# Cross attention in steps of four chunks, each chunk's copy out of PSUM divided by bank between ScalarE and VectorE

## What is computed

```python
# x: (8, 64, 2048), ctx_4096: (8, 1601, 2048), all float32
def _L0_xattn_ref(query, key):
    a = jnp.einsum('bqd,bkd->bqk', query, key)
    e = jax.nn.softmax(a, axis=-1)
    return jnp.einsum('bqk,bkd->bqd', e, key)

x = x + _L0_xattn_ref(_layernorm(x, axis=-1), ctx_4096)
x = x + _L0_attn_ref(_layernorm(x, axis=-1), L0_attn_w_q, L0_attn_w_k, L0_attn_w_v, L0_attn_w_o)
x = x + _L0_ffn_ref(_layernorm(x, axis=-1), L0_ffn_A_w, L0_ffn_B_w, L0_ffn_Wq_w, L0_ffn_keys)
```

## Time and profile before

| | |
|---|---|
| time, median of 3 runs | 1732.3 us (1731.9 to 1732.43) |
| profiled execution | 1732.83 us, of which the span 1731.0 us |
| PE busy | 1671.8 us, 97% |
| DVE busy | 561.0 us, 32% |
| ACT busy | 455.4 us, 26% |
| mean granted clock | 0.991 |

### The profile page before, as it was taken

The page is one execution under the profiler, slowest core; times in us unless marked ns, Lnnn a source line. Parts: engine busy times, 40 slices in busy tenths (PEclk is TensorE's granted clock), DMA queues, the critical chain, the costliest instruction groups (busy, mean ns, idle before and its releaser), DMA issues.

```text
span 1731.0 us, 21539 instructions
## 1 busy us (share of the span) xinstructions
PE 1671.8 (97%) x9037; PEld 1225.1 (71%) x9037; DVE 561.0 (32%) x1018; ACT 455.4 (26%) x630; POOL 372.5 (22%) x95
## 2 busy tenths in 40 slices
PE   4899999999999979999999999999999999999999
PEld 3555555555555538888888888888888788887877
DVE  2444646465463451101202203112012022138423
ACT  1233332332333232231121221222212212232221
POOL 0000000000001002344344344343343343350010
PEclk9899999999999989999999999999999999999999
DMA  9166675756677533323223323322332342220023
GB/s 339 41 208 189 206 223 172 233 175 217 210 223 230 181 127 122 98 73 97 86 84 97 89 84 95 93 87 84 97 95 75 97 145 74 97 98 25 25 73 122
DMA packets 178882, 224.51 MB, mean 130 GB/s; under 512 B 4240, under 2 KB 102544, under 8 KB 176048
## 3 DMA queue, kind: packets, MB, share of 16 engines
q1 hardware_dynamic: 178816, 223.56, 40.9%
HBM read 212.54 MB, written 11.01 MB: 129 GB/s over the span
## 4 chain that ended last, share of the span: by engine, by line
PE 93%; DVE 2%; SPq 2%; ACT 1%; DMA 1%; issue 1%; DVEq 0%; ACTq 0%
PE ps L761 19%; PE ps L763 18%; PE ps L762 18%; PE ps L635 11%; PE ps L671 10%; PE ps L701 10%; PE ps L1485 2%; SPq L366 2%; PE ps L1599 1%; PE ps L1506 1%; DMA xa_xq<-in_x 1%; PE ps L644 1%; PE ps L1454 0%; PE ps L1492 0%; PE ps L674 0%
## 5 line engine op out<-in xcount | busy, mean ns | idle before, releaser
L1069 POOL TENSOR_TENSOR w_lo<-raw,w_hi 128x2048 fp32r<-128x2048 f32 x75 | 345.1, 4601 | 648.1 <-ACT w_hi L1121 648.1
L761 PE MATMUL ps<-h_hi,w_hi 128*128 128x512 f32 x800 | 316.8, 396 | 0.0
L763 PE MATMUL ps<-h_hi,w_lo 128*128 128x512 f32 x800 | 312.0, 390 | 0.0
L762 PE MATMUL ps<-h_lo,w_hi 128*128 128x512 f32 x800 | 311.7, 390 | 0.0
L1305 DVE TENSOR_TENSOR rows<-rows,ps 128x512 f32<-128x512 f32 x128 | 87.9, 687 | 427.6 <-PE ps L763 427.6
L761 PE MATMUL ps<-w_hi,o_hi 128*128 128x512 f32 x528 | 208.4, 395 | 6.1 <-ACT sa_q_t L1156 4.1
L585 DVE COPY xa_ct<-ps 128x768 f32<-128x768 f32 (+1 forms) x128 | 126.8, 990 | 256.7 <-PE ps L635 172.9
L1121 ACT ACTIVATE w_hi<-raw 128x2048 fp32r<-128x2048 f32 x75 | 143.5, 1913 | 240.4 <-PE ps L763 240.4
L763 PE MATMUL ps<-w_hi,o_lo 128*128 128x512 f32 x528 | 206.2, 391 | 0.0
L762 PE MATMUL ps<-w_lo,o_hi 128*128 128x512 f32 x528 | 206.1, 390 | 0.0
L671 PE MATMUL ps<-xa_ct,xa_q_t 128*64 128x384 f32 x1024 | 202.4, 506 | 0.0
(11 more groups left out here) (205 smaller groups left out, 1529.8 us busy)
## 6 DMA issues: line engine op xcount, KB each, us to landing
xa_raw_a<-in_ctx SPq DMA_DIRECT2D x32, 1536.0 KB
xa_raw_b<-in_ctx SPq DMA_DIRECT2D x32, 1536.0 KB, 6.7
raw<-in_L_attn_w_q SPq DMA_DIRECT2D x32, 1024.0 KB, 5.7
raw<-in_L_attn_w_o SPq DMA_DIRECT2D x30, 1024.0 KB, 5.0
raw<-in_L_attn_w_k SPq DMA_DIRECT2D x8, 1024.0 KB, 5.3
raw<-in_L_attn_w_v SPq DMA_DIRECT2D x8, 1024.0 KB, 5.2
xa_xq<-in_x SPq DMA_DIRECT2D x8, 512.0 KB, 8.4
xa_raw_a<-in_ctx SPq DMA_DIRECT2D x32, 128.0 KB
```

What stands on the lines that cost most here:

```text
L761: pe.matmul(out, hi, mov_hi, start=first, stop=False)
L762: pe.matmul(out, hi, mov_lo, start=False, stop=False)
L763: return pe.matmul(out, lo, mov_hi, start=False, stop=last)
L1069: pool.tensor_tensor(w_lo[:, n, :], raw[:, n, :], w_hi[:, n, :].bitcast(F32), ALU.subtract).then_inc(w_lo_done, 1)
```

## The change

A step has four chunks, a whole piece of 512 features, and there are 64 of them. The four chunks go through the same two units of PSUM: chunk `u` goes to unit `u % 2`, and its transposes wait for the copies of chunk `u` - 2, in the same step for `u` = 2 and 3. Each chunk's copy is divided by bank: ACT copies values 0 to 511, DVE the rest (321 or 256). All side tiles behind a chunk (exponentials, queries) are copied by DVE. `xa_ct` holds four chunks, of one step, and no second place. In a step PE now does T, then P, then S of this same step, and S waits chunk by chunk for the copies.

The side work moves with the steps: the exponentials follow the maxima in the same step, PE transposes them in the next (`PV_AT` = 1), rescale, fold, finish and the copy to `xa_acc` stand in the step of the group's products, and the output's statistics one step later. All four statistics of the next queries stand in step 2 of a batch, the links in 3 and 4, the normalization in 5 and 6, the transposes of the queries in 7.

```diff
-CHUNKS = 2
+CHUNKS, UNITS = 4, 2
-PV_AT = 2
+PV_AT = 1
...
-    ct = sb("xa_ct", [P, 2, CHUNKS, KEYS[0] + 1])
+    ct = sb("xa_ct", [P, CHUNKS, KEYS[0] + 1])
...
 # ScalarE
-                act.wait_ge(t_done[0], evacuations(t))
-                if t < STEPS:
-                    ins = act.activation(ct[:, t % 2, 0, 0:width(t)], ps_t[:, 0, 0:width(t)], ACT.Copy)
-                for dst, src in side_copies(t, 0):
-                    ins = act.activation(dst, src, ACT.Copy)
-                ins.then_inc(first_copied, 1)
+                for u in range(CHUNKS):
+                    act.wait_ge(t_done, chunk_no(t, u) + 1)
+                    act.activation(ct[:, u, 0:512], ps_t[:, u % UNITS, 0:512], ACT.Copy).then_inc(first_copied, 1)
...
-            if i == 1 and 0 <= h < STAGES:
                 exponentials(h)
-            for gh, c in groups_before(t, 1):
+            for gh, c in groups_before(t, 0):
...
 # VectorE
-            if has_transposes(t):
-                dve.wait_ge(t_done[1], evacuations(t))
+            for u in chunks_at(t):
+                dve.wait_ge(t_done, chunk_no(t, u) + 1)
                 if t < STEPS:
-                    ins = dve.tensor_copy(ct[:, t % 2, 1, 0:width(t)], ps_t[:, 1, 0:width(t)])
-                for dst, src in side_copies(t, 1):
+                    ins = dve.tensor_copy(ct[:, u, 512:width(t)], ps_t[:, u % UNITS, 512:width(t)])
+                for dst, src in side_copies(t, u):
                     ins = dve.tensor_copy(dst, src)
                 ins.then_inc(second_copied, 1)
...
-            for gh, c in groups_before(t, 1):
+            for gh, c in groups_before(t, 0):
                 if gh % HALVES == 1:
                     rescale(gh, c)
                     fold(gh, c)
                     finish(gh, c)
-            for gh, c in groups_before(t, 2):
+            for gh, c in groups_before(t, 1):
...
-                if at in STATS_AT:
-                    if at == STATS_AT[0]:
-                        dve.wait_ge(xq_in, 16 * (b + 2))
-                    for c in range(2):
-                        row_stats(2 * (at - STATS_AT[0]) + c)
+                if at == STATS_AT:
+                    dve.wait_ge(xq_in, 16 * (b + 2))
+                    for c in range(NCOL):
+                        row_stats(c)
...
 # TensorE
+            n = chunk_no(t, u)
+            if n >= UNITS:
+                pe.wait_ge(first_copied, n - 1)
+                pe.wait_ge(second_copied, n - 1)
...
+                pe.wait_ge(first_copied, chunk_no(t, u) + 1)
+                pe.wait_ge(second_copied, chunk_no(t, u) + 1)
                 g = CHUNKS * i + u
...
         for t in range(ALL_STEPS):
...
-            if 1 <= t <= STEPS:
-                scores(t - 1)
             for h, n in USE_AT.get(t, []):
                 product(h, n)
+            if t < STEPS:
+                scores(t)
```

More of the change, by code:

```diff
@@ L102, in groups_before @@
     return GROUPS_AT.get(t - ago, [])
-Q_AT = (PER + 5, PER + 6)
+Q_AT = 2 * PER - 1
 def side_transposes():
@@ L112, in side_transposes, with chunk_no, chunks_at, copies_until @@
         t = PER * (h + 1) + PV_AT
[L113 to L118, removed]
+        for j in range(JOINT):
+            at[t, j] = [("e", h, j)]
+        if h % HALVES == 0:
+            at[t, 3] = [("odd", h, 0)]
     for b in range(1, B):
-        for n, i in enumerate(Q_AT):
-            for u in range(CHUNKS):
-                at[HALVES * PER * (b - 1) + i, u] = [("q", b, 8 * n + 4 * u + k) for k in range(4)]
+        for u in range(CHUNKS):
+            at[HALVES * PER * (b - 1) + Q_AT, u] = [("q", b, 4 * u + k) for k in range(4)]
     return at
 SIDE = side_transposes()
[L129 to L144, removed]
-OUT_END = {b: GROUP_STEP[HALVES * b + 1, NCOL - 1] for b in range(B - 1)}
[L146 to L150, removed]
+def chunk_no(t, u):
+    return CHUNKS * min(t, STEPS) + u
+def chunks_at(t):
+    return range(CHUNKS if t < STEPS else JOINT if t == E_LAST else 0)
+def copies_until(what, h, j):
+    return next(chunk_no(t, u) for (t, u), v in SIDE.items() if (what, h, j) in v) + 1
+STATS_AT, CHAIN_AT, NORM_AT = 2, (3, 4), (5, 6)
+OUT_END = {b: GROUP_STEP[HALVES * b + 1, NCOL - 1] for b in range(B - 1)}
+OUT_LINKS_AT = {OUT_END[b] + 1: b for b in range(B - 2)}
+OUT_NORM_AT = {OUT_END[b] + 2: b for b in range(B - 2)}
+STORE_AT = {OUT_END[b] + 3: b for b in range(B - 2)}
+NEXT_AT = {OUT_END[b] + (4 if b < B - 2 else 2): b for b in range(B - 1)}
+WEIGHT_LOAD_AT, WEIGHT_SPLIT_AT = (50, 53), (52, 55)
 @dataclass
@@ L289, in cross_attention @@
     q_ready = sem("xa_q_ready")
-    t_done = [sem(f"xa_t_done{u}") for u in range(CHUNKS)]
+    t_done = sem("xa_t_done")
     first_copied = sem("xa_first_copied")
@@ L466, in cross_scalar @@
             if t in OUT_NORM_AT:
[L467 to L470, removed]
+                b = OUT_NORM_AT[t]
+                act.wait_ge(out_stats, b + 1)
+                for c in range(NCOL):
                     act.wait_ge(stored[c], 16 * (b + 1))
-                part = xr[:, half * D // 2:(half + 1) * D // 2]
-                act.activation(part, part, ACT.Identity, bias=out_rs[:, 4:5], scale=out_rs[:, 0:1]).then_inc(out_norm, 1)
+                act.activation(xr[:], xr[:], ACT.Identity, bias=out_rs[:, 4:5], scale=out_rs[:, 0:1]).then_inc(out_norm, 1)
             if t in WEIGHT_SPLIT_AT:
@@ L569, in out_links, with some @@
             yield from rsqrt_steps(dve, out_rs, out_mv[:, 1:2])
-        def some(links_left):
-            for _ in range(6):
+        def some(links_left, n):
+            for _ in range(n):
                 ins = next(links_left, None)
@@ L617, in cross_vector @@
                 if at in CHAIN_AT:
-                    some(norm)
+                    some(norm, 6)
                 if at in NORM_AT:
@@ L658, in first_queries, with scores @@
             pe.wait_ge(first_q_out, 1)
-        def score_step(t):
+        def scores(t):
             stage, i = divmod(t, PER)
@@ L669, in score_step @@
                 q = q_t[:, b % 2, g, :]
-                keys = ct[:, t % 2, u, :]
+                keys = ct[:, u, :]
                 ins = [pe.matmul(ps_s[side(a), bank, 0:MAIN], q, keys[:, a * MAIN:(a + 1) * MAIN], start=first, stop=last)
@@ L673, in score_step @@
                 if x == 0:
-                    ins[u] = pe.matmul(ps_s[side(u), bank, MAIN:MAIN + ODD], q, keys[:, ODD_AT:ODD_AT + ODD], start=False,
+                    a = u % 2
+                    ins[a] = pe.matmul(ps_s[side(a), bank, MAIN:MAIN + ODD], q, keys[:, ODD_AT:ODD_AT + ODD], start=False,
                                        stop=g >= DC - 2, skip_group_check=True)
-            return ins
-        def scores(t):
-            ins = score_step(t)
-            if t % PER == PER - 1:
+            if i == PER - 1:
                 for a in range(SIDES):
```

77 lines of the change are left out of this document (32 added, 45 removed).

## The result

The changed kernel takes **1746.1 us** (median of 4 runs, 1744.62 to 1747.89) against 1732.18 for the kernel before in the same comparison: a ratio of 1.008, with a 95% interval of 1.0067 to 1.0092. It is slower by 13.9 us; forecast were 17.1 us and 1749.4. The profiled execution took 1744.62 us with a span of 1742.4, so the span grew by 11.4 us.

What follows compares the result with a forecast made beforehand. The prediction took PE's own pace and its turns between blocks as the bound. Its terms, -1 + 26.7 - 6.6 (old wait gone) - 6.5 + 4.5 = +17.1 us on a span of 1731.0, gave 1749.4 us, range 1728 to 1768.

Steps and rivals of the forecast that it cites:

- DVE's waits: PE waits for DVE's copies queued behind its side work: 4.45 us a batch in batches 1 to 6, +26.7 us.
- place 3: Step 3 of a batch's eight four-chunk steps, numbered 0 to 7; PE's third chunk was to wait 2.2 us there.
- place 4: Step 4 of a batch's eight, numbered 0 to 7; PE's third chunk was to wait 0.95 us there.
- place 5: Step 5 of a batch's eight, numbered 0 to 7; PE's third chunk was to wait 1.3 us there.
- The start: First batch: more chunks transposed and scored before DVE stands at the second batch's rows, shortening PE's standstill: -6.5 us.
- The clock: Granted clock falls behind the roughly 2 us wait in step 3, in half of six batches: +4.5 us.
- rival 2: Clock falls at most DVE waits, also those of a microsecond: 15 to 18 times 1.5, 1768 to 1772 us; chance 0.17.
- Blocks and turns: PE's transposes, scores, products and the turns between them; with the third-chunk hold counted, -1 us for all.
- The hold: PE's third chunk waits for ACT's copy of the first: 0.21 us, or 0.26 with six tiles a chunk.
- rival 1: PE loses nothing inside a four-chunk step, no hold or turns: about 24 us saved, 1725 us; chance 0.13.
- Rival 3: DVE's waits half as long, engines falling in step: 13 instead of 26.7, no clock fall, 1731 to 1736 us; chance 0.14.
- Rival 4: Long transpose runs bring the clock down in every four-chunk step: 60 x 1.5 = 90, 1840 us; chance 0.04.

Runs made afterwards that it cites:

- the first experiment: The changed kernel with DVE's statistics, links and normalization of a step moved ahead of its rescales: 1716.8 us, ratio 0.9906.
- the second: The changed kernel with two of the four rows of input statistics moved from step 2 to step 0, except in the first batch: 1732.5 us, ratio 0.9994.
- the start alone: The changed kernel with the first batch's input statistics and links one step later: 1739.84 us, ratio 1.0037.
- Products inside the transposes: The changed kernel with PE's products moved between second and third chunk in steps 2, 3, 6 and 7 of a batch: 1730.48 us, ratio 0.9978.
- without the division by bank: The kernel with DVE's side work ahead of rescales (1716.8 us), ACT copying even chunks whole and DVE odd ones: 1736.58 us, ratio 1.0028.
- the last kernel: The 1716.8 us kernel (DVE's side work ahead of rescales) plus later first-batch statistics, early ACT copy release, second half of links in step 5: 1703.63 us.

## Why the prediction was right

**DVE's waits**, the term that decided, came where they were put and nearly as long: 2.2 forecast and 2.21 measured in place 3, 0.95 and 1.08 in place 4, 1.3 and 1.42 in place 5; 26.7 and 28.4 in all. The count from the start of P held step by step: in place 2 P begins at 190.66, PE's next restart was put 9.5 later, and it came at 200.11, 9.45 later. It could be counted so closely because every row of DVE's side work stands in the trace of before, and an in-order queue adds them. By moving that work and nothing else, the first experiment takes the waits away but for 0.83 us in place 5, and the second halves the longest.

**The start**: -6.5 forecast, -6.7 measured, by the mechanism given; moving the statistics once more gave 6.3. That the size came so close is in part luck, because two things that the sum did not have cancel: the rows landed 0.95 us later than before (46.03 against 45.08), and PE worked 3.7 us at a granted clock of 0.50 behind the standstill (49.17 to about 52.9) instead of 5.5 (47.43 to about 52.9), worth 0.9.

**The clock**: three falls of 1.5 were forecast, four of 1.61 came in the profiled run, all behind the wait in place 3. The waits of 1.08 and 1.42 brought none, so rival 2 is out. Which of six like waits brings one no run here explains; in the profiled run of the start alone it was the same four batches.

**Blocks and turns** was mis-sized: forecast -1 in all, measured -1.11 a batch, some -8. A batch without its waits takes 77.49 - 4.73 = 72.76, that of before 74.98 - 1.11 = 73.87. The lengths of T were right (3.20 and 3.02 against 3.21 and 3.02). The step that failed is the turn from S to the next T, taken at 0.15 from the earlier trace rows. After, PE in place 2:

```profile
264.94 3.27 PE L621 MATMUL ps<-ident,xa_raw_a 128*128 128x128 f32 x28
268.14 2.80 PE L688 MATMUL ps<-xa_raw_b,xa_e_t 128*64 128x512 f32 x12
270.77 0.81 PE L662 MATMUL ps<-xa_ct,xa_q_t 128*64 128x384 f32 x4
...
273.73 1.49 PE L621 MATMUL ps<-ident,xa_raw_a 128*128 128x128 f32 x12
```

P takes 2.63 and S 2.96, together 5.59, where 2.58 + 2.92 + 0.15 = 5.65 were put; S of the second half takes 2.68 without any turn, where 2.83 was put. The 0.15 came from an S that had transposes on both sides. Products inside the transposes give such an S again: it took 3.02 there, against 2.97 behind P, so a part of the 0.15 belongs to the turn from T into S, which the new order hasn't got. This alone would have put the forecast 7 us too high; the waits (1.7 more than forecast) and the falls (1.9 more) took half of it back.

**The hold** had the right length by a half-right cause. ACT's copy ends it, as put, but by little: DVE's would end it only some 0.01 earlier (258.96 against 258.97 in the rows above): the prediction dismissed DVE's share as shorter, with one estimate of 0.1 from a copy's end to PE, where the traces have 0.05 for ACT and 0.15 for DVE. So rival 1, too, named the wrong point from which it would decide: with ACT's copy released before chunk 1 is through, most of the hold of 28 tiles stayed. Of the 0.50 and 0.55 a double step that it promised beyond the count, 0.06 (8.80 against 8.86) and at most 0.15 (T and S of the second half 5.70 against 5.85) came.

**Rival 3**, waits half as long because the engines fall in step, fell by the eighteen waits that keep their lengths to 0.01 from batch to batch. **Rival 4** fell too: while PE did nothing but transposes for 3.4 us, the granted clock was 1.00. After, place 7, the transposes of keys and queries:

```profile
237.20:240.60 3.40, 3.40 (x31) 2.75 (x30) 2.26 (x6) 1.79 (x3) 0.00 (x0) 1.00 1.02 379
```

The Trainium skill, "TensorE: Matmul & The Clock Gate", Part 4, says that the clock's full level doesn't engage for transposes. The trace disagrees where the clock was at the full level already, with that row. Transposes alone also raised it from the lower one. In the kernel of the start alone, PE's first work is the 14 transposes of the first two chunks and the 16 of the queries; beside them the queries' transposes of after:

```profile
10.88 2.97 PE L621 MATMUL ps<-ident,xa_raw_a 128*128 128x128 f32 x14 [10.88 <-DMA xa_raw_a<-in_ctx]
13.78 1.22 PE L645 MATMUL ps<-ident,xa_xq 64*128 64x64 f32 x16
```

```profile
13.70 1.97 PE L645 MATMUL ps<-ident,xa_xq 64*128 64x64 f32 x16
```

The 14 took 2.90 us, where 14 take 1.58 at a granted clock of 1.00: they ran at the lower level. (The trace has no record of the granted clock before its first change, so the pace stands for it.) The 16 behind them took 1.22 us here and 1.97 in after, whose clock rose only during the first scores. The rise came before PE had done anything but transposes in four of the ten traces.

Chance had a part as well: the fall of the clock near the end of the kernel, 1.5 to 1.8 us, stood in the profile of before and not in that of after, and it is no work of the change.

## What to carry to other kernels

When an engine makes copies that another engine waits for and has other work as well, count in its in-order queue how much of that work stands between the event that makes the copy possible and the copy; a longer step gathers that work in one place, and the copy waits for all of it. Put ahead the work that needs nothing of the present step, and behind it what waits for the step anyway: here that order alone turned +14 us into -16. Only then ask what the larger step saves in turns, and whether a copy split between two engines ends at the same moment on both, counted up to where the waiting engine goes on.

## What was not expected of the hardware

- Of six waits of 2.21 us in the same place, four brought the granted clock down to 0.50 for some three microseconds (1.61 us each) and two did not; the waits of 1.03 to 1.43 us in the batches of these kernels brought it down nowhere. A wait of 2.21 us thus cost 2.2 or 3.8 us, and those of half its length themselves alone. At the start, a wait of 1.65 us (to 16.65 in the kernel of the start alone) had the clock at 0.50 behind it, from 17.1 on, in the three traces in which it had risen by then.
- From the end of a copy out of PSUM to the restart of PE the traces have 0.05 us after ACT (264.11 to 264.16 without the division by bank) and 0.15 us after DVE (199.96 to 200.11 in after).
- The second batch's rows landed at 46.03 us after the span's start in after, 44.77 to 48.31 in the experiments (46.95 in the start alone, 47.70 in the last kernel), against 45.08 before; the end of the standstill at the start moves with them, so a term of the start cannot be measured to better than one or two microseconds here.
